# A top-128 search: the last count on VectorE, and TensorE builds the two candidate lists in PSUM

## The reference

```
draft = jnp.einsum('bhqd,bhkd->bhqk', qr, kr)
draft = draft + jnp.where(causal_future, neg, jnp.asarray(0.0, dtype))
_, draft_indices = jax.lax.top_k(draft, num_remain)          # num_remain = 128
mask = mask.at[b_idx, h_idx, s_idx, draft_indices].set(0.0)
mask = jnp.where(causal_future[None, None, :, :], neg, mask)
scores = jnp.einsum('bhqd,bhkd->bhqk', qr, kr) / np.sqrt(HD).astype(np.float32) + mask
attn = jax.nn.softmax(scores, axis=-1)
out = jnp.einsum('bhqk,bhkd->bhqd', attn, v)
```

## Time and profile before

| | us |
|---|---|
| median of 3 runs (lowest, highest) | 2386.71 (2383.52, 2387.93) |
| the profiled execution's own time | 2377.4 |
| its span, first to last instruction | 2375.6 |
| the loop over the tiles, first start (L1323) to the last tile's start | 1160 to 2099 |
| TensorE, VectorE, ScalarE, GpSimd busy over the span | 72%, 68%, 54%, 43% |

### The profile page before, as it was taken

The page is one execution under the profiler, slowest core; times in us unless marked ns, Lnnn a source line. Parts: engine busy times, 40 slices in busy tenths (PEclk is TensorE's granted clock), DMA queues, the critical chain, the costliest instruction groups (busy, mean ns, idle before and its releaser), DMA issues. The chain is left out here.

```text
span 2375.6 us, 25955 instructions
## 1 busy us (share of the span) xinstructions
PE 1707.7 (72%) x7274; PEld 1270.8 (53%) x7274; DVE 1615.9 (68%) x3711; ACT 1293.2 (54%) x3343; POOL 1017.7 (43%) x699
## 2 busy tenths in 40 slices
PE   5899998999898699998655433652545553387997
PEld 4777777777777578876422222331322222245885
DVE  3777777777776545656338898879779888822435
ACT  3555656556555332334167878776787778252221
POOL 3445545545444256552012344545434434632442
PEclk9999999999999799998556667775767776687998
DMA  4112111111111122212300000200000000001111
GB/s 151 32 43 91 41 50 56 67 57 54 60 41 58 54 80 104 82 53 99 58 7 7 7 8 1 27 7 1 8 7 7 7 7 1 1 0 45 48 45 49
DMA packets 33570, 96.40 MB, mean 41 GB/s; under 512 B 4048, under 2 KB 16720, under 8 KB 29264
## 3 DMA queue, kind: packets, MB, share of 16 engines
q1 hardware_dynamic: 33456, 95.20, 12.2%
HBM read 87.84 MB, written 7.34 MB: 40 GB/s over the span
## 5 line engine op out<-in xcount | busy, mean ns | idle before, releaser
L198 PE MATMUL PS<-XT,AR 128*128 128x512 f32 x2472 | 617.6, 405 | 26.0 <-POOL AR L805 12.3
L198 PE MATMUL PS<-AR 128*128 128x512 f32 (+2 forms) x2568 | 552.2, 370 | 100.4 <-issue 69.8
L198 PEld LDWEIGHTS PS<-AR 128*128 128x128 f32 x2568 | 449.5, 195 | 196.3 <-issue 91.5
L198 PEld LDWEIGHTS PS<-XT,AR 128*128 128x128 f32 x2472 | 469.4, 192 | 138.4 <-issue 16.8
L1244 POOL TENSOR_TENSOR AF<-AF 128x512 f32<-128x512 f32 (+3 forms) x64 | 148.5, 2320 | 487.7 <-DVE AF L1449 487.7
L1185 ACT ACTIVATE AF<-PS 128x512 f32<-128x512 f32 x160 | 94.0, 594 | 255.8 <-PE PS L1065 134.5
L1052 PE MATMUL PS<-AR,XT 48*128 48x128 f32 (+3 forms) x256 | 127.5, 498 | 142.4 <-DVE BF L1312 74.7
L1080 PE MATMUL PS<-AF,BF 128*128 128x512 f32 x320 | 191.6, 703 | 20.7 <-ACT AF L1185 20.5
L1100 PE MATMUL PS<-BF,AF 128*128 128x1 f32 x24 | 7.0, 362 | 264.3 <-DVE BF L1410 264.3
L559 POOL TENSOR_TENSOR AF<-AF 128x512 f32<-128x512 f32 (+1 forms) x64 | 107.6, 1681 | 167.8 <-DVE AF L690 167.8
L553 POOL TENSOR_TENSOR AF<-AF 128x512 f32<-128x512 f32 x80 | 103.3, 1292 | 168.2 <-ACT AF L345 168.2
(11 more groups left out here) (171 smaller groups left out, 3616.0 us busy)
## 6 DMA issues: line engine op xcount, KB each, us to landing
AF<-in_mean_w SPq DMA_DIRECT2D x48, 448.0 KB, 3.3
AF<-in_ffn_w SPq DMA_DIRECT2D x14, 1536.0 KB, 6.5
AF<-in_attn_w SPq DMA_DIRECT2D x9, 1536.0 KB, 6.4
AF<-in_attn_w SPq DMA_DIRECT2D x9, 1024.0 KB, 5.0
AF<-in_ffn_w SPq DMA_DIRECT2D x11, 769.0 KB, 4.4
XT<-rope_scratch SPq DMA_DIRECT2D x96, 64.0 KB, 2.7
rope_scratch<-BF SPq DMA_DIRECT2D x20, 256.0 KB, 2.3
AF<-in_x SPq DMA_DIRECT2D x8, 256.0 KB, 3.8
```

The source lines that it names most:

```text
L198: last = nc.tensor.matmul(dst, lhs(a, c), rhs(m, c), start=(first and k == 0), stop=(k == 3 * n - 1 and not more))
```

## The change

Rounds 0 to 2 stay on ScalarE, in another order among its other work. The fourth count becomes a VectorE compare (`mark`): 1.0 where the score is at or above the threshold, 0.0 elsewhere, in bf16, with its sum. The GpSimd pass `below`, the VectorE pass L1379 and both match_replace go. TensorE rebuilds each head's scores twice in PSUM (`lists`): once with -2^126 added at the marks, so that the 8 largest are those just below the threshold, and once negated with -2^126 added everywhere and +2^126 at the marks, so that the 8 largest are those just above it. VectorE takes max of both directly from PSUM (`pick`). For the second product the keys (negated by GpSimd, `negate`) and the queries lie a second time in SBUF rows 64 to 111, so SyncE now issues 12 transfers for a tile's queries and 6 for each half of a batch's keys. All of a tile's lists need its queries, so the next load into that buffer waits for the lists, not for the scores. The aim moves from 120 to 128 above the threshold, and the constant `PRIOR` from 8 to 100. Scores and lists share a ring of four PSUM banks. The core of the diff:

```diff
-AIM = TOPK - (WINDOW + 1) // 2
+SIDE = (WINDOW + 1) // 2
+AIM = TOPK
+BIG = 2.0 ** 126
+NONE = 99.0
 ROUNDS = 4
-PRIOR = 8.0
...
+        def scored(x, h):
+            return 16 * x + 32 * before(x - 1) + h
+        def listed(x, h, side):
+            return 16 * min(x + 2, NB) + 32 * before(x) + 2 * h + side
+        def keys_read(x):
+            return (listed(x, 15, 1) if tile_of(x)[1] > 0 else scored(x, 15)) + 1
...
-            for n in range(TT):
-                b, i = n // QT, tile_of(2 * n)[1]
+            for x in range(NB):
+                n, i, hf, W = tile_of(x)
+                b = n // QT
+                if x >= 2:
+                    sp.wait_ge(A1["ring_full"], keys_read(x - 2))
                 if n % QT == 0:
-                    if b > 0:
-                        sp.wait_ge(A1["scores"], QT * 32)
-                    for a, s in enumerate((0, 1, 0)):
-                        src = scr[b, 4, s].rearrange("(c h) t -> c h t", c=HD1)
-                        sp.dma_start(f32(kst[a * HD1:(a + 1) * HD1]), src).then_inc(A1["kst"], 16)
-                for x in (2 * n, 2 * n + 1):
-                    if x >= 2:
-                        sp.wait_ge(A1["scores"], 16 * (x - 1))
+                    for low in (0, 64):
+                        for a, s in enumerate((0, 1, 0)):
+                            src = scr[b, 4, s].rearrange("(c h) t -> c h t", c=HD1)
+                            sp.dma_start(f32(kst[low + a * HD1:low + (a + 1) * HD1, 4 * hf:4 * hf + 4]),
+                                         src[:, 4 * hf:4 * hf + 4]).then_inc(A1[f"kst{hf}"], 16)
+                for low in (0, 64):
                     for j in range(2):
                         for a, s in enumerate((0, 0, 1)):
-                            src = scr[b, 2 * (x % 2) + j, s].rearrange("(c h) t -> c h t", c=HD1)
-                            sp.dma_start(f32(qst[a * HD1:(a + 1) * HD1, x % 2, 8 * j:8 * j + 8]),
+                            src = scr[b, 2 * hf + j, s].rearrange("(c h) t -> c h t", c=HD1)
+                            sp.dma_start(f32(qst[low + a * HD1:low + (a + 1) * HD1, x % 2, 8 * j:8 * j + 8]),
                                          src[:, :, i * P:(i + 1) * P]).then_inc(A1[f"qst{x % 2}"], 16)
...
+            def slot(k):
+                wait(pe, A1["ring_free"], k - 3)
+                return PS[:, k % 4]
             def scores(x, q):
                 n, i, hf, W = tile_of(x)
                 if q == 0:
-                    pe.wait_ge(A1["kst"], 48 * (n // QT + 1))
-                    pe.wait_ge(A1[f"qst{x % 2}"], 16 * 6 * (x // 2 + 1))
-                for h in range(G1):
-                    head = hf * 16 + 4 * q + h
-                    wait(pe, A1["evac"], 16 * x + 4 * q + h - 3)
-                    nc.tensor.matmul(PS[:, h, 0:W], qst[0:48, x % 2, 4 * q + h, :], kst[0:48, head // G1, 0:W],
+                    pe.wait_ge(A1[f"kst{hf}"], 96 * (n // QT + 1))
+                    pe.wait_ge(A1[f"qst{x % 2}"], 16 * 12 * (x // 2 + 1))
+                for h in range(4 * q, 4 * q + 4):
+                    dst = slot(scored(x, h))
+                    nc.tensor.matmul(dst[:, 0:W], qst[0:48, x % 2, h, :], kst[0:48, 4 * hf + h // G1, 0:W],
                                      start=True, stop=False)
-                    nc.tensor.matmul(PS[:, h, W - P:W], ident_r, mask_r, start=False, stop=True)\
-                        .then_inc(A1["scores"], 1)
+                    nc.tensor.matmul(dst[:, W - P:W], ident_r, mask_r, start=False, stop=True)\
+                        .then_inc(A1["ring_full"], 1)
+            def lists(x, h):
+                n, i, hf, W = tile_of(x)
+                q, k = qst[:, x % 2, h, :], kst[:, 4 * hf + h // G1, 0:W]
+                mark = above[:, h % 3, 0:W]
+                pe.wait_ge(A1["above"], 16 * before(x) + h + 1)
+                dst = slot(listed(x, h, 0))
+                nc.tensor.matmul(dst[:, 0:W], negbig_b, mark, start=True, stop=False)
+                nc.tensor.matmul(dst[:, W - P:W], ident_r, mask_r, start=False, stop=False)
+                nc.tensor.matmul(dst[:, 0:W], q[0:48], k[0:48], start=False, stop=True).then_inc(A1["ring_full"], 1)
+                if h % 8 == 0:
+                    pe.wait_ge(A1["kneg"], 2 * (n // QT) + hf + 1)
+                dst = slot(listed(x, h, 1))
+                nc.tensor.matmul(dst[:, 0:W], ident_b, less_big[:, 0:W], start=True, stop=False)
+                nc.tensor.matmul(dst[:, 0:W], big_b, mark, start=False, stop=False)
+                nc.tensor.matmul(dst[:, 0:W], q[64:112], k[64:112], start=False, stop=True).then_inc(A1["ring_full"], 1)
...
             for x in range(-1, NB + 2):
                 xp = x - 1
+                if 0 <= xp < NB and tile_of(xp)[1] > 0:
+                    for h in range(16):
+                        lists(xp, h)
                 if x + 1 < NB:
                     scores(x + 1, 0)
                 if xp >= 1 and (xp - 1) % 2:
...
-            def count(x, r, heads=range(16)):
...
+            def count(x, r):
                 n, i, hf, W = tile_of(x)
                 act.wait_ge(A1["thr"], ROUNDS * before(x) + r + 1)
-                first = 16 * (ROUNDS * before(x) + r)
-                for h in heads:
-                    if r < ROUNDS - 1:
-                        wait(act, A1["acc"], first + h - 1)
-                        place = junk[h % 2]
-                    else:
-                        k = 8 * (before(x) - 1) + h // 2
-                        if h % 2 == 0:
-                            wait(act, A1["below"], k + 1)
-                        else:
-                            wait(act, A1["below_odd"], 2 * k + 1)
-                        place = sgn[:, h, :]
-                    nc.scalar.activation(place[:, 0:W], S1[x % 2][:, h, 0:W], ACT.Sign,
+                first = 16 * ((ROUNDS - 1) * before(x) + r)
+                for h in range(16):
+                    wait(act, A1["acc"], first + h - 1)
+                    nc.scalar.activation(junk[h % 2][:, 0:W], S1[x % 2][:, h, 0:W], ACT.Sign,
...
+                if shown:
+                    exp(xp, 0)
                 if search:
-                    for r in range(1, ROUNDS - 1):
-                        count(x, r)
-                if 0 <= xp < NB:
-                    exp(xp, 0)
+                    count(x, 1)
+                if shown:
                     exp(xp, 1)
-                    last_round(6)
+                if search:
+                    count(x, 2)
+                if shown:
                     act.wait_ge(A1["tau"], xp + 1)
-                    pt(xp, 0, last_round)
+                    pt(xp, 0)
                     exp(xp, 2)
-                    last_round()
-                    pt(xp, 1, last_round)
+                    pt(xp, 1)
                     exp(xp, 3)
-                    last_round()
-                    pt(xp, 2, last_round)
-                    last_round(2)
-                    pt(xp, 3, last_round)
-                last_round(16)
+                    pt(xp, 2)
+                    pt(xp, 3)
...
+            def negate(b, hf):
+                k = kst[64:112, 4 * hf:4 * hf + 4]
+                pool.wait_ge(A1[f"kst{hf}"], 96 * (b + 1))
+                nc.gpsimd.tensor_scalar(k, f32(k), -1.0, None, ALU.mult).then_inc(A1["kneg"], 1)
+                pool.wait_ge(A1["kneg"], 2 * b + hf + 1)
+            negate(0, 0)
+            negate(0, 1)
...
+                if r < 2:
+                    v.tensor_tensor(t, t, st["step"], ALU.add).then_inc(A1["thr"], 1)
+                else:
+                    v.scalar_tensor_tensor(st["thr"], t, -1.0, st["step"], ALU.mult, ALU.subtract).then_inc(A1["thr"], 1)
+            def mark(x, h):
...
+                v.tensor_scalar(above[:, h % 3, 0:W], S1[x % 2][:, h, 0:W], st["thr"][:, h:h + 1], 0.0,
+                                ALU.is_ge, ALU.add, accum_out=acc[:, 2, h:h + 1]).then_inc(A1["above"], 1)
+            def pick(x, h):
+                W = tile_of(x)[3]
+                for side in range(2):
+                    k = listed(x, h, side)
+                    dve.wait_ge(A1["ring_full"], k + 1)
+                    v.max(best[:, h, SIDE * side:SIDE * side + SIDE], PS[:, k % 4, 0:W]).then_inc(A1["ring_free"], 1)
...
+                missing, below, over = st["square"], st["err"], st["scaled"]
+                rows = missing.unsqueeze(2).to_broadcast([P, 16, 16])
+                dve.wait_ge(A1["above"], 16 * (before(x) + 1))
+                step(v.tensor_scalar(missing, acc[:, 2], -1.0, float(TOPK), ALU.mult, ALU.add))
+                step(v.tensor_tensor(hit, at_tau.unsqueeze(1).to_broadcast([P, 16, 16]), rows, ALU.is_equal))
+                dve.wait_ge(A1["ring_free"], listed(x, 15, 1) + 1)
+                step(v.tensor_tensor(val, hit, best, ALU.mult))
+                step(v.tensor_reduce(below, val[:, :, 0:SIDE], AX.X, ALU.add))
+                step(v.tensor_reduce(over, val[:, :, SIDE:2 * SIDE], AX.X, ALU.add))
```

(25 more changed lines are left out.)

141 lines of the change are left out of this document (53 added, 88 removed).

## The result

The changed kernel takes 2545.89 us (median of 4 runs, 2517.97 to 2552.9) against 2385.11 before (2382.81 to 2387.93): a ratio of 1.0652, 95% interval 1.0571 to 1.0733. It is slower, as forecast, but 59 us above the forecast of 2487 and outside its range of 2447 to 2535. The profiled execution (2552.9 us) is the longest of the four and has a span of 2551.1 us. Its first `start` is 6.1 us later than before; from there to the last `start` it takes 1109.8 us where it took 939.0, 170.8 more. The steps of the prediction put 97 into this stretch. So 74 us are to be explained.

A forecast was written before the change was run, and what follows sets the result against it. VectorE was taken as busiest, waiting for ScalarE. From 2377.4 us, +158 + 14 + 4 + 11 - 32 - 32 - 12 - 10 = +101 gave 2478, a median of 2487; range 2447 to 2535.

The forecast's parts named there:

- The load: Query transfers now wait for the last list; VectorE waits for projection and flag behind the scores: +158 us, keys +14.
- The projection: In odd steps it runs on TensorE after the scores, at a clock mostly risen: 3.5 us each.
- The keys: In steps 7 and 8 six key transfers stand ahead of the queries: 7 us more, twice, 14 us.
- Counts: ScalarE has 48 Sign passes a tile instead of 64, so VectorE's waits ahead of the updates shrink: -32 us.
- `cut`: On VectorE it becomes ten instructions instead of eight, 3.6 to 3.7 us each time: +11 us over 12 tiles.
- the first load: More key and query transfers before the first scores make the first load 4 us later.
- max from PSUM: VectorE's max on lists in PSUM costs 0.61 us for 512, as from SBUF; nothing added.
- `final`: VectorE's waits ahead of it shrink as the third update lies inside them: -12 us, from 0 to -30.
- GpSimd beside VectorE: `below` no longer slows small instructions of `start`: -10 us; `negate` lies beside work that doesn't wait for GpSimd.
- Picks: VectorE's mark and two max take 1.83, 1.43 and 1.03 us a head with 512, 384 and 256 keys.
- TensorE's side per head, at full clock: Lists on TensorE take 1.6 to 2.0 us a head for 512 keys, 1.3 to 1.7 for 384, 1.1 to 1.5 for 256.
- rival 2: TensorE stays at clock 0.50 through the lists, 3.2 us a head for 512 keys, 2.1 for 256: 2700 us, 5%.

The follow-up runs named there:

- run 1: Changed kernel with a third buffer for the queries, so their load no longer waits for the previous tile's lists: 2426.2 us, ratio 1.0159.
- run 2: Changed kernel with projection and flag ahead of the next tile's first four heads of scores on TensorE: 2416.9 us over ten runs, ratio 1.0092 without the two highest.
- run 10: The changed kernel measured once more, nothing edited: 2520.4 us, ratio 1.0602.
- run 9: Measurement only: changed kernel with four blocks of 16 matmuls, with and without row turns, ahead of each step's first list: 2695.4 us, one execution.
- run 6: Changed kernel with eight wide matmuls ahead of each step's first list, plus one ahead of each list in 256-key tiles: 2527.0 us, ratio 1.059.
- run 4: Changed kernel with eight extra matmuls of 512 bf16 columns ahead of each tile's first list: 2528.5 us, ratio 1.0601.
- run 12: Changed kernel with third query buffer, projection and flag first, negation on VectorE, grouped list matmuls, and eight wide matmuls ahead of each first list: 2350.1 us, ratio 0.985.
- run 8: Changed kernel with third query buffer, projection and flag first, negation on VectorE, and list matmuls grouped by rows: 2342.3 us, ratio 0.9811.
- run 5: Changed kernel with each head's list matmuls grouped, four of 128 rows and then two query products of 48 rows: 2483.9 us, ratio 1.0395.
- run 11: Changed kernel with the negation of the keys on VectorE instead of GpSimd, no other edit: 2518.2 us, ratio 1.0567.

## Why the prediction was wrong

**The load: right as a sum, by luck in its parts.** 172 us worked out, 176.5 measured. The wait for the queries was 9.7 (9.71) us. Two parts were off and cancel. The projection was to take 3.5 us, because "the clock will have risen for most of it"; it took 4.3 to 5.4, at a granted clock of 0.51 to 0.67, so the odd steps cost some 10 us more. The keys were to cost 7 us in each of steps 7 and 8; TensorE waited 4.6 and 4.3 longer there and VectorE 3 and 4, so 7 in all and not 14. Odd steps waited 17.0 to 18.6 us, and 21.0 in step 7; even ones 8.9 to 10.1, and 13.7 in step 8. Runs 1 and 2 take the term away in two ways: the two waits fall by 116 and by 151 us, of which 32 come back in run 2.

**Counts, `cut`, the first load, max from PSUM: right.** The counts' waits gave 31 us (32). `cut` takes 3.73 us (3.6 to 3.7). The first load cost 6 (4). The 65 ns more for each max that the sentence on the Trainium skill weighed ("VectorE: DVE Perf Modes", TRN2 errata) did not appear: 0.605 us from PSUM.

**`final`: too small.** The waits ahead of it fell by 20 us, not 12.

**GpSimd beside VectorE: two steps wrong, and the total right by luck.** "lies beside work that doesn't wait for GpSimd" holds for semaphores, but VectorE's small instructions stood still beside `negate`: 4.1 us in each of two steps, 8 in all. That `below` is gone from beside `start` was worth 17 us, not 10. So `start` gave 9.3 us where 10 were worked out. And one price is missing: the third update now stands behind `final` q = 2, where GpSimd's `norm` runs beside it in three steps of 12:

```profile
1652.69 3.60 POOL L1268 TENSOR_TENSOR AF<-AF 128x2048 f32<-128x2048 f32 x1 [5.17 <-DVE AF L1468]
```

```profile
1654.73 1.60 DVE L1378 TENSOR_TENSOR BF<-BF 128x16 f32<-128x16 f32 x1
```

L1378 takes 1.60, 1.60 and 2.91 us there instead of 0.16; that is 5.5 us in all.

**Picks: the step that failed** is "TensorE's side per head, at full clock", together with the 5% for rival 2 and its reason, that "it comes to the lists straight from such work". The clock was at its low level in 6 of 12 tiles in the first profile and in 4 in run 10. Only in step 3 had TensorE been at 0.50 already; in the others it came at clock 1.00, and the clock fell after the lists had begun. Rival 2 was half true: true for the tiles with 256 keys, sometimes true for wider ones, and at 1.99 us a head near its price of 2.1 (2.88 with 512 keys, where it had 3.2). With VectorE's own 1.83, 1.43 and 1.03, the paces 1.85, 1.55 and 1.33 had 16 x 4 x (0.02 + 0.12 + 0.30) = 28 us of waits for lists in them. Measured were 78: +50. VectorE's own head was 1.86, 1.50 and 1.08: +10. Another 15 I have not split up; in part it is that a max of 256 that had to be waited for costs its whole 0.43 us, and 0.34 behind another. And the old picks had cost 343 us, not the 335 of the pairs that were read: -8. So +67. Most of it goes with the low clock: two wide tiles at 1.00 made run 10's profile 33 us shorter. Its 2520 us lie inside the range, so on these two tiles it hung whether the time would; the step failed in both profiles.

**The sum.** VectorE's time, from each start to the next and with its waits, adds up to the whole 170.8 us. Against the prediction's 97: picks +67, the load +6 (with `resolve`'s other waits), the update +5.5, `start`, `cut` and counts +3, `final` -6.5 (with its reciprocal), all else -1.6. That makes the 74.

The turn itself was priced well (0.2 each with the queries, 0 to 0.2 with bf16; a pair of turns costs 0.30 at full clock, 0.41 at half). At the full clock a head of 256 keys would take 1.2 us by this, an estimate from 1408 columns (0.59) and four turns of run 9 (0.6), and not 1.33. What was missing is that these lists do not keep the full clock. The Trainium skill says of turns ("TensorEngine Tiling (Array Packing)", Key Properties) that a change of the tiling mode drains TensorE, while different tiles can load and multiply in parallel. Run 9's times fit both, if a product of 48 rows runs in another mode than one of 128, which no record of the trace names: 0.52 against 0.23 us for a pair that changes row counts, 0.12 for one on two row groups.

**Open.** Why the clock falls while TensorE counts as busy is not settled: it stays low through the turning in run 9, wide products among the lists avoid it in run 6 and wide products ahead of them raise it in runs 4 and 12. Yet in three steps of run 9 it fell before the first turn, the same turning lists stayed at 1.00 in tiles where they had to wait for VectorE, and runs 8 and 12 have 0.83 to 0.95 in wide tiles that had 1.00 before. Each run's clock is read from one profile. No run took the turns away and left all else: run 5 halves them and also lets two products run side by side.

## What to carry to other kernels

When a wait moves behind a long loop, price everything queued behind the waiting instruction, and try the cheap cure first: one line of order on TensorE was worth some 119 us, as much as a third buffer. When work moves on VectorE or GpSimd, look what small instructions it comes to lie beside. When short matmuls of different row counts take turns, group them by rows, and put independent 48-row products on two row groups next to each other. And take a time at the full clock only for matmuls that the trace shows at the full clock in the same mixture; where TensorE is the slower side, price both levels.

## What the runs showed of the hardware

Two fp32r products of 48 rows on rows 0 to 47 and 64 to 111, in two PSUM banks, start within 0.01 us of each other and take as long as one (0.12 us a pair with 256 columns, 0.23 on one row group). A round trip between 48-row and 128-row weights costs 0.30 us at clock 1.00. TensorE's granted clock can be 0.51 over 47 us in which the profile has it 98% busy. Beside a GpSimd `tensor_scalar` of 5.37 us a VectorE `tensor_tensor` of 128x16 took 3.61 us, and 0.19 in run 11, where the other is gone; beside a GpSimd `tensor_tensor` of 3.60 us one took 1.60 to 2.91 instead of 0.16.
